# Routing and experts of an attention and mixture-of-experts kernel in one block, with GpSimd clearing row buffers

## The reference

```python
x = L0_attn_x
x = x + _L0_attn_ref(_layernorm(x), Wq, Wk, Wv, Wo)
x = x + _L0_ffn_ref(_layernorm(x), w_cls, bias, w_gate_up, w_down)

# _L0_ffn_ref, E = 32 experts, Z = 32 "zero" experts, K = 8, I = 256, CAP = 256
scores = softmax(xf @ w_cls.T)
_, topk_idx = top_k(scores + bias, K)
w = take(scores, topk_idx); w = w / (w.sum() + EPS) * 1.5
w_r, w_z = w of the chosen experts below E, and of the others
# per expert e: the rows of the tokens that chose it, at most 256
g, u = split(rows @ w_gate_up[e], 2)
y = (silu(g) * u) @ w_down[e]
out = sum over a token's experts of w_r * y, times (1 + w_z.sum())
```

## Time and profile before

| | us |
|---|---|
| median of 3 runs | 958.33 |
| lowest and highest | 957.64, 958.46 |
| the profiled execution | 956.62 |
| its span, first to last instruction | 954.7 |

### The profile page before, as it was taken

One profiled execution on the slowest core, in us unless ns is written; L12 is line 12 of the kernel. 1 busy time (PEld: TensorE's weight loads), 2 busy tenths in 40 slices (PEclk: granted clock), 3 DMA queues, 4 the chain that ended last, 5 costly groups with the idle time before them and its releaser, 6 DMA issues. The chain is left out here.

```text
span 954.7 us, 14619 instructions
## 1 busy us (share of the span) xinstructions
PE 909.0 (95%) x4432; PEld 737.1 (77%) x4432; DVE 772.3 (81%) x1843; ACT 503.3 (53%) x867; POOL 475.7 (50%) x395
## 2 busy tenths in 40 slices
PE   5899999999999999999999999999998999999995
PEld 3677888888888888888877888888875767767784
DVE  6988888888888888888987777777766789888882
ACT  5455555556545554465556222333223588787782
POOL 1466766667666676666650000000002767676852
PEclk9999999999999999999999999999999999999998
DMA  9011111111111111111185477443217889899942
GB/s 316 7 34 50 39 53 59 45 50 42 59 50 46 49 54 47 50 45 40 58 307 171 143 275 260 162 136 131 94 47 275 233 267 336 253 297 317 327 61 40
DMA packets 67367, 127.05 MB, mean 133 GB/s; under 512 B 12072, under 2 KB 14504, under 8 KB 65232
## 3 DMA queue, kind: packets, MB, share of 16 engines
q1 hardware_dynamic: 58144, 114.67, 34.4%
q0 software_dynamic: 9136, 11.31, 6.6%
HBM read 106.53 MB, written 32.90 MB: 146 GB/s over the span
## 5 line engine op out<-in xcount | busy, mean ns | idle before, releaser
L615 POOL TENSOR_TENSOR a_t<-a_t 128x512 f32<-128x512 f32 x80 | 105.0, 1313 | 98.7 <-DVE a_t L378 98.7
L624 POOL TENSOR_TENSOR a_fQ<-a_fQ,a_den 128x512 f32<-128x512 f32 x64 | 88.0, 1374 | 71.8 <-DVE a_den L416 71.8
L213 PE MATMUL a_PQ<-w_h,a_xT_h 128*128 128x512 f32 x384 | 108.0, 404 | 7.7 <-DVE w_l L365 7.7
L1093 POOL TENSOR_SCALAR r_vr<-r_mv 128x1 f32<-128x1 f32 x16 | 8.4, 524 | 195.8 <-DVE r_mv L918 195.8
L802 PE MATMUL r_PY<-w_h,r_o_h 128*128 128x512 f32 x256 | 105.0, 410 | 0.0
L213 PE MATMUL a_PQ<-w_l,a_xT_h 128*128 128x512 f32 x384 | 104.3, 394 | 0.0
L213 PE MATMUL a_PQ<-w_h,a_xT_l 128*128 128x512 f32 x384 | 103.6, 392 | 0.0
L802 PE MATMUL r_PY<-w_h,r_o_l 128*128 128x512 f32 x256 | 100.5, 393 | 0.0
L412 DVE CUSTOM_DVE_ANT_0 a_m<-a_fQ,a_z 128x128 f32<-128x128 f32 x256 | 100.3, 444 | 0.0
L1240 POOL DMA_INDIRECT m_xg<-xn2d,si x64 | 75.9, 1187 | 48.7 <-DVE m_xg L1377 17.5
L802 PE MATMUL r_PY<-w_l,r_o_h 128*128 128x512 f32 x256 | 99.8, 390 | 0.0
(11 more groups left out here) (190 smaller groups left out, 2266.4 us busy)
## 6 DMA issues: line engine op xcount, KB each, us to landing
oT<-a_o SPq DMA_DIRECT2D x64, 256.0 KB, 2.4
v_l<-in_wgu SPq DMA_DIRECT2D x32, 512.0 KB, 6.3
raw<-in_wgu SPq DMA_DIRECT2D x24, 512.0 KB, 5.8
v_l<-oT SPq DMA_DIRECT2D x11, 1024.0 KB, 7.3
v_l<-in_wd SPq DMA_DIRECT2D x16, 512.0 KB, 6.9
raw<-in_wd SPq DMA_DIRECT2D x12, 512.0 KB, 5.8
v_h<-oT SPq DMA_DIRECT2D x5, 1024.0 KB, 6.7
out<-r_x SPq DMA_DIRECT2D x18, 256.0 KB, 2.0
```

The source lines that it names most:

```text
L213: last = eng.matmul(bank[:, :], a[:, k, :], w[:, 4 * i + k, :], start=s == 0 and k == 0, stop=s == 2 and k == 3)
L615: eng.tensor_tensor(t1[:, r % 2, :], t1[:, r % 2, :], t2[:, r % 2, :], ALU.add).then_inc(sm["xr"], 1)
L624: eng.tensor_tensor(q, q, den[:, n % 2, :].unsqueeze(2).broadcast_to([P, 4, P]), ALU.mult).then_inc(sm["fs"], 1)
```

## The change

`routing` and `experts` return their five functions instead of opening a block, and one block calls them one after the other on each engine, so the barrier between them is gone. What the barrier guaranteed is now told by waits: GpSimd waits for all stores of routing and for `si` before its first gather. GpSimd also clears the buffers of experts 0 to 2 (six buffers of 128x544), behind its last `rstd` and once the last `project` is done, since these buffers now lie where routing's `o_l` was. VectorE clears expert 3 after `si` is written, and 4 and 5 where it did before. Besides:

- the two stores to the spare rows of `out` go from the end of routing into chunk 3, and the residual of chunk 5 and later odd chunks waits for them too;
- the identity for `turn` is loaded in chunk 5 instead of at the begin of experts;
- after the last `project` SP loads expert 3 alone ahead of the last `store_w`, then 4; the loads of 5 move behind the first gather of expert 1, ahead of 6;
- ScalarE splits the weights of expert 1 and loads its table for Silu in routing;
- 12 filler matmuls instead of 16 stand ahead of the first `turn`, in another PSUM bank.

```diff
@@ routing, SP
+                if c == 3:
+                    for t in range(2):
+                        eng.dma_start(out[T + t * P:T + (t + 1) * P, :], x2[:, 1, :]).then_inc(sm["r_so1"], 16)
                 if c == 5:
                     load_up(sm, eng, ring, wgu, 7)
-                for t in range(2):
-                    eng.dma_start(out[T + t * P:T + (t + 1) * P, :], x2[:, 1, :]).then_inc(sm["r_so1"], 16)
+                    eng.dma_start(ident0[:, :], consts[:, 0:128]).then_inc(sm["m_id"], 16)
                 eng.wait_ge(sm["r_y"], NC)
-                for e in (3, 4):
-                    load_up(sm, eng, ring, wgu, e)
-                    load_down(sm, eng, ring, wd, e)
+                load_up(sm, eng, ring, wgu, 3)
+                load_down(sm, eng, ring, wd, 3)
                 store_w(NC - 1)
-                load_up(sm, eng, ring, wgu, 5)
-                load_down(sm, eng, ring, wd, 5)
-                for b in range(2):
-                    eng.wait_ge(sm[f"r_so{b}"], 16 * (NC // 2 + 2 * b))
-                    eng.wait_ge(sm[f"r_sx{b}"], 16 * (NC // 2))
-                    eng.wait_ge(sm[f"r_sw{b}"], 16 * (NC // 2))
+                load_up(sm, eng, ring, wgu, 4)
+                load_down(sm, eng, ring, wd, 4)
@@ routing, DVE
-                        eng.wait_ge(sm[f"r_so{c % 2}"], 16 * (c // 2))
+                        eng.wait_ge(sm[f"r_so{c % 2}"], 16 * (c // 2 + 2 * (c % 2 and c >= 5)))
...
+                eng.scalar_tensor_tensor(out=si[:, :], in0=ids, scalar=-1.0, in1=id0[:, :], op0=ALU.add,
+                                         op1=ALU.add).then_inc(sm["r_tt"], 1)
+                eng.wait_ge(sm["r_tt"], 2)
@@ routing, ACT
+                for part in range(3):
+                    split_high(sm, eng, ring, w_h_, 1, part)
+                eng.wait_ge(sm["m_id"], 16)
+                eng.activation(warm[:, :], ident0[:, 0:1], ACT.Silu)
@@ routing, POOL
                 for c in range(NC):
                     rstd(c)
+                eng.wait_ge(sm["r_y"], NC)
+                for e in range(3):
+                    for t in range(2):
+                        eng.memset(xg[:, e, t, :], 0.0).then_inc(sm["r_ve"], 1)
+                for b in range(2):
+                    eng.wait_ge(sm[f"r_so{b}"], 16 * (NC // 2 + 2 * b))
+                    eng.wait_ge(sm[f"r_sx{b}"], 16 * (NC // 2))
+                    eng.wait_ge(sm[f"r_sw{b}"], 16 * (NC // 2))
+                eng.wait_ge(sm["r_tt"], 2)
@@ experts, SP
-                eng.dma_start(ident[:, :], consts[:, 0:128]).then_inc(sm["m_id"], 16)
                 eng.wait_ge(sm["m_g01"], 16)
+                load_up(sm, eng, ring, wgu, 5)
+                load_down(sm, eng, ring, wd, 5)
                 load_up(sm, eng, ring, wgu, 6)
@@ experts, POOL, gather
                     if e >= 6:
                         eng.wait_ge(sm[f"m_a{t}"], e - 5)
+                    elif e >= 3:
+                        eng.wait_ge(sm["m_xg"], i - 5)
                     else:
-                        eng.wait_ge(sm["m_xg"], i + 1)
+                        eng.wait_ge(sm["r_ve"], NC + i + 1)
@@ experts, PE
-                run_on(PG[0], 16)
+                eng.wait_ge(sm["m_wh"], 1)
+                run_on(PY[0], 12)
@@ experts, DVE
-                for e in range(4):
+                for e in range(3, 4):
                     clear(e, 0)
                     clear(e, 1)
@@ experts, ACT
-                w_high(1, (0, 1))
-                eng.wait_ge(sm["m_id"], 16)
-                eng.activation(warm[:, :], ident[:, 0:1], ACT.Silu)
                 load_flag(eng, regs, 0)
                 both(eng, regs, 0, x_high, "m_xTh1")
-                w_high(1, (2,))
```

More of the change, by code:

```diff
@@ L648, in _, with routing @@
                         rstd(c + 1)
-def routing(nc, sm, x, wo, wc, bias, consts, oT, xn2d, out, si, ring, wgu, wd, w_h_, w_l_, v_h, v_l):
+def routing(nc, sm, x, wo, wc, bias, consts, oT, xn2d, out, si, ring, wgu, wd, w_h_, w_l_, v_h, v_l, xg, ident0, warm):
     with ExitStack() as ctx:
@@ L1162, in experts @@
         a_l = sb("a_l", [P, 2, 256], F32R)
+        sb("rows", [P, 6, 2, XW])
         y = [sb("y0", [P, 6, D]), sb("y1", [P, 4, D])]
@@ L1167, in experts @@
         low = sb("low", [P, 2, 512], F32R)
-        ident = sb("ident", [P, P])
         full = sb("full", [1, 64], U32)
-        warm = sb("warm", [P, 1])
         PX = [ps("PX0"), ps("PX1")]
@@ new lines, in on_gpsimd, with gather, scatter @@
+        def on_gpsimd(eng):
+            regs = flags(eng, "mp")
+            def gather(e, t):
+                i = 2 * e + t
+                if e >= 6:
+                    eng.wait_ge(sm[f"m_a{t}"], e - 5)
+                elif e >= 3:
+                    eng.wait_ge(sm["m_xg"], i - 5)
+                else:
+                    eng.wait_ge(sm["r_ve"], NC + i + 1)
+                eng.indirect_dma_start(
+                    xg[:, e % 6, t, :], None, xn2d[:, :],
+                    bass.IndirectOffsetOnAxis(ap=si[:, i:i + 1], axis=0),
+                    bounds_check=T - 1, oob_is_err=False).then_inc(sm[f"m_g{t}{e % 6}"], 16)
+            def scatter(e, t, rows, done, last):
+                i = 2 * e + t
+                if t == 0 and e >= 1:
+                    eng.wait_ge(sm["m_s"], 32 * e)
+                eng.wait_ge(sm[f"m_y{t}"], e + 1)
+                eng.indirect_dma_start(
+                    out[:, :], bass.IndirectOffsetOnAxis(ap=si[0:rows, i:i + 1], axis=0),
+                    y[t][0:rows, e % deep[t], :], None, compute_op=ALU.add,
+                    engine_sem=sm["m_sent"] if last else None).then_inc(sm["m_s"], done)
+            for e in range(6):
+                gather(e, 0)
+                gather(e, 1)
+            asked = 6
+            for e in range(NE):
+                ahead = e + 7 + (e >= 3) + (e >= 8)
+                while asked < min(ahead, NE):
+                    gather(asked, 0)
+                    gather(asked, 1)
+                    asked += 1
+                if e == 0:
+                    eng.wait_ge(sm["m_full"], 1)
+                load_full(eng, regs, e)
+                with eng.If_lt(regs[e % 7], T):
+                    scatter(e, 0, P, 16, False)
+                    scatter(e, 1, P, 16, True)
+                with eng.Else():
+                    scatter(e, 0, 64, 32, True)
```

1078 lines of the change are left out of this document (527 added, 551 removed).

## The result

| | before | after |
|---|---|---|
| median, us | 958.32 | 963.28 |
| lowest to highest of 5 runs | 957.64 to 958.46 | 962.63 to 966.61 |
| profiled execution | 956.62 | 966.61 |
| its span | 954.7 | 964.7 |

The ratio of the times is 1.006, with a 95% interval of 1.0042 to 1.0079. The forecast was 958.9 with a range up to 962.0, so it was too low by 4.4 us.

A forecast was written before the change was run, and what follows sets the result against it. Experts runs at TensorE's pace, so its first turn of gathered rows sets the end: -2.50 us (barrier and clears gone) and +3.10 (memsets holding VectorE's `normal`) make +0.6, so 958.9 us, range 955.4 to 962.0.

The follow-up runs named there:

- f2: The changed kernel with an unused 32-byte buffer behind `warm`, memsets not delayed: 970.16 us, 1.0049 of the kernel before.
- f3: The changed kernel with a 32-byte buffer behind `warm` and GpSimd's six memsets behind VectorE's last `normal`: 966.46 us, 1.0021 of the kernel before.
- g1: The changed kernel with a 96-byte buffer behind `warm`, memsets not delayed: 964.53 us, 1.0026 of the kernel before.
- g2: The changed kernel with a 96-byte buffer behind `warm` and GpSimd's six memsets behind VectorE's last `normal`: 964.25 us, 1.0027 of the kernel before.
- i2: The changed kernel with memsets behind VectorE's last `normal`, `warm` behind all other buffers, 16 fillers instead of 12: 960.32 us, 0.9949 of the kernel before.

## What to carry to other kernels

Put work on an idle engine behind, not beside, the short VectorE step on which the tail hangs; here one wait was worth 3.1 us in the first group and cost nothing. (With other addresses the same wait was worth 3.7 between f2 and f3, and 0.3 between g1 and g2, of 6 runs each, where the clock of g1 had stayed up anyway.) Look at which buffers an edit moves, not only at which instructions: two small allocations ahead of the operands of all products of routing and experts cost more than the barrier that the change removed, and a profile shows it as the same source line at a new median in a stretch that nobody touched. When a delay makes TensorE idle for longer than it ever was, count a slower clock behind it as likely: four of the five profiles with a wait of 3.5 us had it, and one didn't.

## What the hardware showed beside that

- **Start addresses.** The 128x512 matmuls of `w_l` with `r_o_h` had a median of 389 ns where both operands start 128 bytes behind a multiple of 256, and of 393 to 395 with `r_o_h` 32, 64 or 128 bytes beyond that, in all 20 profiles without exception.
- **A row of GpSimd memsets isn't one block for VectorE.** It got in between the third and fourth in two profiles and between the fourth and fifth in one. The row of six then took 0.29 or 0.28 us longer, which is about the 0.28 from the end of the memset ahead to the end of VectorE's instruction.
- **ScalarE stands still at its first activations in experts** on four of the five chips of the experiments, in every profile of either structure, and neither on the first nor in the profiles of before and after. From i2:

```profile
747.37 0.38 ACT L1444 ACTIVATE m_a<-m_PG 128x256 f32<-128x256 f32 x1 [5.20 <-remote]
750.94 0.60 ACT L1421 ACTIVATE m_xT_h<-m_PX 128x512 fp32r<-128x512 f32 x1 [3.19 <-remote]
```

With it the stretch from the first turn to the end takes 222 to 225 us instead of 217 to 221, and most of the difference between the chips' medians of the kernel before (957.7 against 962.2 to 964.5) is of that size. Its cause wasn't looked for.
